# A mixed fp32 block kernel on one core: k's values and squares interleaved by transfers, one pass of products for the k features, and a new order of each batch on every engine

## The reference

```python
mod = (silu(c) @ wmod).reshape(16, 6, 1, 128)        # sa, ca, ga, sb, cb, gb of each batch
h = layernorm(x) * (1 + ca) + sa
# attention with 16 heads of 8 dimensions and M = 32 random features:
#   feature(u) = (exp(u @ orf.T / 8**0.25 - sum(u*u) / (2*8**0.5)) + 1e-6) / sqrt(32)
q, k = feature(h @ Wq.T + bq), feature(h @ Wk.T + bk);  v = h @ Wv.T + bv
out = q @ (k.T @ v) / (q @ sum(k))                    # per batch and head
x = x + ga * (out @ Wo.T + bo)
h = layernorm(x) * (1 + cb) + sb
e = argmax(h @ gate_W + gate_b)                       # one of 8 experts for each row
x = x + gb * (gelu(h @ W1[e] + b1[e]) @ W2[e] + b2[e])
```

## Time and profile before

| | |
|---|---|
| device time, median of 3 runs | 381.62 us (381.19 to 385.29) |
| span of the profiled execution | 360.6 us |
| median less that span | 21.0 us |
| TensorE busy with matmuls, share of the span | 94% |
| TensorE weight loads | 73% |
| VectorE, ScalarE, GpSimd | 75%, 74%, 59% |
| bytes moved by transfers | 60.47 MB, 168 GB/s |

### The profile page before, as it was taken

One profiled execution on the slowest core, in us unless ns is written; L12 is line 12 of the kernel. 1 busy time (PEld: TensorE's weight loads), 2 busy tenths in 40 slices (PEclk: granted clock), 3 DMA queues, 4 the chain that ended last, 5 costly groups with the idle time before them and its releaser, 6 DMA issues.

```text
span 360.6 us, 13729 instructions
## 1 busy us (share of the span) xinstructions
PE 338.8 (94%) x4823; PEld 263.9 (73%) x4823; DVE 271.2 (75%) x1104; ACT 265.1 (74%) x644; POOL 213.2 (59%) x262
## 2 busy tenths in 40 slices
PE   6899999899988999998999999999999999999994
PEld 5445765566465566646665669999989999999993
DVE  3456997898879789878887978887677676666653
ACT  2688988799878888977888756676656667666761
POOL 3142386776667757857854618846767455545554
PEclk9999999999999999999999999999999999999999
DMA  7174656774566547444432467445657665545410
GB/s 233 50 253 166 210 184 221 259 243 160 177 227 205 176 167 230 163 132 156 153 133 100 149 163 227 142 118 150 194 161 269 209 184 147 147 128 135 137 38 12
DMA packets 40211, 60.47 MB, mean 168 GB/s; under 512 B 5426, under 2 KB 28086, under 8 KB 40016
## 3 DMA queue, kind: packets, MB, share of 16 engines
q1 hardware_dynamic: 33776, 42.54, 39.9%
q0 software_dynamic: 6368, 17.05, 12.5%
HBM read 28.63 MB, written 19.34 MB: 133 GB/s over the span
## 4 chain that ended last, share of the span: by engine, by line
PE 60%; ACT 15%; DMA 10%; DVE 6%; issue 5%; POOL 1%; SPq 1%; DVEq 1%; POOLq 0%; ACTq 0%
PE ps_proj L1350 16%; PE ps_feat L1337 9%; DMA qmix<-qsqs 9%; PE ps_proj L1132 6%; PE ps_den_gate L1337 4%; PE ps_proj L1182 4%; PE ps_kv L1337 4%; ACT qf L627 3%; ACT qvals L606 2%; ACT shared L588 2%; PE ps_kv L1198 2%; PE ps_out L1330 2%; ACT den L656 2%; ACT shared L581 2%; ACT kvm L600 2%
## 5 line engine op out<-in xcount | busy, mean ns | idle before, releaser
L545 POOL DMA_INDIRECT out<-kf,modb x71 | 70.1, 987 | 52.4 <-DVE kf L1060 47.0
L507 POOL DMA_INDIRECT experts_lists<-pay,slot x64 | 65.9, 1030 | 43.4 <-DVE slot L893 29.5
L1350 PE MATMUL ps_proj<-w2sb,qf 128*128 x568 | 75.0, 275 | 0.4 <-ACT qf L690 0.4
L1350 PEld LDWEIGHTS ps_proj<-w2sb,qf 128*128 128x128 f32 x568 | 68.9, 192 | 0.6 <-issue 0.6
L681 ACT ACTIVATE xT<-ps_out 128x128 f32<-128x128 f32 x71 | 19.7, 277 | 44.8 <-PE ps_out L1330 44.1
L1055 DVE TENSOR_TENSOR kf<-ps_proj,firsts_sb 128x128 f32<-128x128 f32 x71 | 20.7, 291 | 34.6 <-PE ps_proj L1350 22.6
L690 ACT ACTIVATE qf<-ps_feat,shared 128x128 f32<-128x128 f32 x144 | 40.9, 374 | 0.0
L1337 PE MATMUL ps_feat<-xT,shared 128*128 128x128 f32 x288 | 38.8, 277 | 1.5 <-issue 0.9
L1337 PEld LDWEIGHTS ps_feat<-xT,shared 128*128 128x128 f32 x288 | 35.0, 192 | 2.8 <-issue 1.7
L1132 PE MATMUL ps_proj<-shared,wsb 128*128 128x512 f32 x62 | 33.3, 620 | 1.0 <-ACT shared L581 0.4
L977 DVE COPY shared<-firsts_sb 128x516 f32 x71 | 31.4, 442 | 1.6 <-issue 1.5
(11 more groups left out here) (189 smaller groups left out, 890.3 us busy)
## 6 DMA issues: line engine op xcount, KB each, us to landing
modb<-experts_lists SPq DMA_DIRECT2D x71, 196.0 KB, 2.8
xall<-in_x SPq DMA_DIRECT2D x16, 256.0 KB, 3.0
pay<-modb SPq DMA_DIRECT2D x16, 256.0 KB, 3.0
qmix<-qvals SPq DMA_DIRECT2D x30, 128.0 KB
qmix<-qsqs SPq DMA_DIRECT2D x30, 128.0 KB
modb<-modulation_rows SPq DMA_DIRECT2D x4, 768.0 KB, 5.2
firsts_sb<-in_firsts SPq DMA_DIRECT2D x8, 322.0 KB, 4.2
w2sb<-in_w SPq DMA_DIRECT2D x8, 256.0 KB
```

What stands on the lines that cost most here:

```text
L507: g_.indirect_dma_start(out=lists, in_=pay[b.home][:, t, :], in_offset=None, out_offset=bass.IndirectOffsetOnAxis(ap=slot[b.home][:, t:t + ...
L545: g_.indirect_dma_start(out=rows_out, in_=yb[u], in_offset=None, out_offset=bass.IndirectOffsetOnAxis(ap=token, axis=0), bounds_check=last ...
L1350: ins = mm(Y[u % 2][:, 0:D], g[u % R4][:, c * P:(c + 1) * P], w2sb[:, bass.ds(e * DFF + c * D, D)], start=(c == 0), stop=(c == FC - 1))
```

## The change

- k's weights are permuted as q's are, ACT's `kvals` and `ksqs` are interleaved by four transfers (`mix_k(v)` on SP) into a new buffer `kmix`, and `k_features` makes 32 products of 64 columns, 32 partitions x 128 rows stationary, in one pass. Batch 0 keeps the two passes.
- k of batch b is projected into G (for b from 2 on), the bank of den. The projection waits for the attention of batch b-2, and the transpose of kvT into G waits for k's values and squares.
- v of batch b is projected and copied in turn b-1.
- Each engine's turn has a new order, in POOL's `rstd1_of` goes first, in SP's turn v `mix_k(v)` stands first and `mix_q(v)` last, behind `gate_rows(v)` and `load_w2`. The rest of POOL's turn is as before.
- The last batch has its own lists.

```diff
@@ sync
             for v in range(1, B):
-                mix_q(v)
+                mix_k(v)
                 if v + EARLY_ROWS + 1 < B:
                     load_x_behind(v + EARLY_ROWS + 1)
...
                     gate_rows(v)
                 if 5 <= v < 5 + E:
                     load_w2(v - 5)
+                mix_q(v)
+            def mix_k(v):
+                sp.wait_ge(s_kst, 2 * v + 1)
+                for n in range(2):
+                    sp.dma_start(kmix[n::2, n, :], kvals[n::2, :]).then_inc(s_kmix, 16)
+                sp.wait_ge(s_kst, 2 * v + 2)
+                for n in range(2):
+                    sp.dma_start(kmix[1 - n::2, n, :], ksqs[n::2, :]).then_inc(s_kmix, 16)
@@ gpsimd
+                if ahead and b.par == 0:
+                    rstd1_of(b.half + 3, b=b + 2)
                 if not first:
                     rstd2_of(b + -1, rows_of=None if second else b + -2)
-                if ahead and b.par == 0:
-                    rstd1_of(b.half + 3, b=b + 2)
@@ scalar, the turn of a middle batch
+                k_pair(b, 0)
+                modulate(b + 1)
+                k_pair(b, 1)
+                if not second:
+                    h2T_copy(b + -2)
+                k_values(b + 1)
+                k_squares(b + 1)
+                q_pair(b, 0)
+                if not second:
+                    gateT(b + -2)
+                q_pair(b, 1)
+                kvm_copy(b)
+                v_values(b + 1)
+                q_values(b + 1)
+                q_squares(b + 1)
+                rden_first(b)
                 if b.v + 2 < B:
                     normalise1(b + 2)
@@ vector, the whole turn of a middle batch as it now stands (statistics of x ahead of it)
                 residual(b + -1)
                 second_stats(b + -1)
                 centre_h2(b + -1)
                 kv_values(b, first)
                 normalise1(b + 2, lo=LT // 2)
                 experts(b + -2)
                 eps_values(b)
                 scale_h2(b + -1)
                 slots(b + -2)
                 attention(b)
@@ tensor
+            def k_features(b):
+                pe.wait_ge(s_kmix, 64 * b.v)
...
+                for t in range(LT):
+                    for n in range(2):
+                        for c in range(NC):
+                            at = slice(c * CW, (c + 1) * CW)
+                            ins = mm(QB[c][:, t * P + n * HP:t * P + (n + 1) * HP], kmix[at, n, t * P:(t + 1) * P],
+                                     feat_q[at, n, :], start=True, stop=True)
@@ tensor, the turn of a middle batch
+                k_features(b)
+                if not second:
+                    transpose_h2(b + -2, first=b.v == 2)
+                transpose_xn(b + 1)
+                out_project(b + -1)
+                project_k(b + 1)
+                q_features(b)
+                kv_product(b)
+                if not second:
+                    gate(b + -2)
+                project_v(b + 1)
+                kv_transpose(b)
+                if not second:
+                    gate_transpose(b + -2)
+                project_q(b + 1)
+                eps_and_den(b)
+                if not second:
+                    rank(b + -2, first=b.v == 2)
+                numerator(b)
```

More of the change, by code:

```diff
@@ L635, in gateT, with rden_first @@
                 a.activation(lgT[:], I[:, 0:P], ACT.Copy).then_inc(s_lgT, 1)
[L637 to L653, removed]
+            def rden_first(b):
                 act.wait_ge(s_den, b.v + 1)
@@ L658, in batch, with first_batch, last_batch @@
                 a.activation(rden[:], den[:], ACT.Exp, scale=-1.0).then_inc(s_rden, 1)
-                if not last:
-                    q_squares(b + 1)
+            def first_batch(b):
+                k_pair(b, 0)
+                k_pair(b, 1)
+                v_values(b)
+                q_pair(b, 0, first=True)
+                modulate(b + 1)
+                q_pair(b, 1, first=True)
+                k_values(b + 1)
[5 more added lines that the diff above has]
+                rden_first(b)
+                normalise1(b + 2)
+            def last_batch(b):
+                k_pair(b, 0)
+                h2T_copy(b + -2)
+                k_pair(b, 1)
+                gateT(b + -2)
+                q_pair(b, 0)
+                q_pair(b, 1)
+                kvm_copy(b)
+                rden_first(b)
+            def batch(b, first=False, second=False, last=False, ahead=True):
+                if first:
+                    return first_batch(b)
+                if last:
+                    return last_batch(b)
+                k_pair(b, 0)
+                modulate(b + 1)
+                k_pair(b, 1)
+                if not second:
+                    h2T_copy(b + -2)
+                k_values(b + 1)
+                k_squares(b + 1)
+                q_pair(b, 0)
+                if not second:
+                    gateT(b + -2)
+                q_pair(b, 1)
+                kvm_copy(b)
+                v_values(b + 1)
+                q_values(b + 1)
+                q_squares(b + 1)
+                rden_first(b)
                 if b.v + 2 < B:
@@ L1001, in batch @@
                     second_stats(b + -1)
+                if second:
+                    dve.wait_ge(s_mb, 16)
+                if b.v > EARLY_ROWS and (b.v - 1 - EARLY_ROWS) % LATE_ROWS == 0:
+                    dve.wait_ge(s_mbl, 16 * ((b.v - 1 - EARLY_ROWS) // LATE_ROWS + 1))
+                if not first and not last:
+                    centre_h2(b + -1)
                 if last:
                     table_rows(0)
-                    kv_values(b)
+                kv_values(b, first)
+                if last:
                     experts(b + -2)
@@ L1008, in batch @@
                     copy_firsts(0)
-                elif not first and not second:
+                if b.v + 2 < B:
+                    normalise1(b + 2, lo=LT // 2)
+                if not first and not second and not last:
                     experts(b + -2)
[L1011 to L1018, removed]
                 eps_values(b)
                 if not first and not last:
-                    centre_h2(b + -1)
                     scale_h2(b + -1)
+                if not first and not second and not last:
+                    slots(b + -2)
                 if b.v == B - 2:
@@ L1140, in v_project, with first_k_features @@
                              start=True, stop=True)
[L1141 to L1149, removed]
+                ins.then_inc(s_pv, 1)
+            def first_k_features(b):
+                pe.wait_ge(s_kst, 2)
                 for t in range(LT):
@@ L1278, in batch @@
             def batch(b, first=False, second=False, last=False, ahead=True):
-                third = b.v == 2
+                if first:
+                    return first_batch(b)
                 if last:
[L1281 to L1288, removed]
+                    return last_batch(b)
@@ L1289, in batch @@
+                k_features(b)
+                if not second:
+                    transpose_h2(b + -2, first=b.v == 2)
+                transpose_xn(b + 1)
+                out_project(b + -1)
+                project_k(b + 1)
+                q_features(b)
+                kv_product(b)
+                if not second:
                     gate(b + -2)
-                q_features(b, first)
-                if not first and not second:
+                project_v(b + 1)
+                kv_transpose(b)
```

138 lines of the change are left out of this document (83 added, 55 removed).

## The result

The changed kernel takes 535.88 us (534.52 to 537.39) against 382.63, a ratio of 1.400 (95% interval 1.392 to 1.409): 153 us slower, where 170 were forecast.

A forecast was written before the change was run, and what follows sets the result against it. TensorE, busy for 338.8 of 360.6 us, was taken as the bound. Loop 151, clock 19, start 3, less 2 of idle time, sum to 171 us; 381.6 + 171 = 553, stated as 552, range 520 to 590.

The forecast's parts named there:

- The step that decides: SP's order: `mix_q` behind `gate_rows` and its scatter wait makes a loop, 151 us over the turns v = 3 to 15.
- The terms of the round: Stretches from one `q_features` through eps product, slots, scatter, `gate_rows` and q's transfers to the next: 24.3 us against 12.4.
- from the squares to `q_features`: Transfer of q's squares, from their issue on SP to TensorE's use of them: 4.54 us per turn.
- The range: Whole kernel: 520 to 590 us, from the ends of the scatter-to-`gate_rows` stretch, q's transfers and the clock.
- Step 6: End of the round: issue of q's values 1.2 us, then squares to `q_features` 4.54; 4.1 to 5.9 in all.
- the low ends: Smallest values of the uncertain terms in the 13 stalled turns: a turn costs 10.7 us more.
- The clock: TensorE falls to 1.2 GHz in each stall and loses 1.5 us: 13 x 1.5 = 19 us, between 0 and 39.
- The k pass: TensorE's k products take 1.8 us instead of 2.1, paced by stationary loads; gain 0.3 per turn, at most 1.1.
- The start and end: Turn 1 loses 3 us to uncovered k transfers; turns 1 and 2 may lose 1 us of idle time each.
- Span and median: The 21.0 us between profiled span and median time were left as they are for the changed kernel.
- The rival of the orders alone: SP's wait is harmless and wo paces the new order: 0.3 to 2 us per turn, 385 to 410; chance 0.03.

The follow-up runs named there:

- before_qmix_last: The kernel before with only `mix_q` moved last in SP's turn, behind `gate_rows` and `load_w2`: 507.86 us, ratio 1.322.
- qmix_first: The changed kernel with `mix_q` moved right behind `mix_k`, ahead of the wait of `gate_rows` for the scatter: 432.81 us, ratio 1.124.
- before_again: The kernel before, unchanged, profiled again beside the others: one execution, 388.19 us, span 386.3.
- gates_later: As qmix_first, with `gate_rows` one turn later, for batch v-1 in SP's turn v: 404.52 us, ratio 1.054.
- gated_first: As gates_later, with POOL making wo ahead of all four scatters instead of behind two: 403.18 us, ratio 1.054.
- slots_earlier: As gates_later, with DVE's `slots` ahead of `scale_h2`: 378.71 us beside 362.45 of the kernel before, ratio 1.044.
- wide_again: keep_warm_wide once more, on one chip with narrow_again: 518.58 us beside 383.79 of the kernel before, ratio 1.345.
- narrow_again: The changed kernel with 150 idle products of 128 columns in the stall, repeated beside wide_again: 527.62 us, ratio 1.376.
- keep_warm_wide: The changed kernel with 39 idle products of 512 columns in the stall: 491.53 us beside 362.45 of the kernel before, ratio 1.353.

## Why the prediction was right

**The step that decides** was right as it stood: `mix_q` behind the wait of `gate_rows`, 13 stalls, a loop through slots, scatters and the last tile. before_qmix_last makes 124 of the 153 us with that line alone, qmix_first takes 103 away with it.

**The terms of the round**, forecast and measured in the round shown: eps product 4.9 plus 1.5 for the clock, measured 6.6 (4.5 when the clock holds), then 2.8 to slots for my 2.8; tile 3 at 14.1 plus 1.5, measured 15.8; to `gate_rows` 3.1, measured 2.6; `gate_rows` and `load_w2` 1.34 and 1.35; q's values 1.2 and 1.2; from the squares to `q_features` 4.54, measured 2.87. This last is the mis-sized one. I took it from a single turn of the kernel before, and a long one: over the 14 turns of that profile it is 3.25 to 4.79, 3.9 on average. Loads of x and of the experts' weights and TensorE's work stood beside that transfer; which of them made it longer was not separated. It takes 1.7 x 13 = 22 us off the sum, and the landing of the scatter another 0.5 x 13 = 6.

**The range.** Step 6 measured 1.23 + 2.87 = 4.1, which is the low end that I gave it. But the turn at the low ends, 10.7 us over the one before, doesn't follow from these ends: 11.6 less 0.5 and 1.6 is 9.5, and the range should have begun near 506. It did no harm, as the measured turn is 10.9 to 11.4 over, by which steps it is counted.

**The clock** fell as said. It costs 2.1 us per turn, 27 us, against 19 forecast, within the bounds. The 1.5 us was a guess that a row only half supports: the pace of products at the start was low for 3 us, but the granted clock of those windows is 1.00. In the stalls it is 0.50 for at least 3 us behind `q_features`, and in four of the 13 turns for 5. Filling the stall gave back up to 5.5% of the kernel before (1.400 to 1.345), about 21 us.

**The k pass**: forecast 1.8, measured 1.94 without gaps, and no gain from half the columns. That the gain would be 0.3 per turn was too much, it is 0.06. In 11 of its 15 turns the changed kernel's pass has gaps and takes 2.4 to 3.5 us; under the stall this costs nothing.

**The start and end**: 3 us less 2 us forecast, 9.0 measured up to `q_features` of batch 2. TensorE waits 3.2 us for k's transfers in turn 1, the cost that I named, and 2.6 for q's in turn 2; what makes up the rest I did not separate.

**Luck.** The errors went both ways: transfer and landing took 28 us off, the clock and the start put 8 each back. So 552 came nearer to 536 than its terms deserved.

**Span and median.** I carried 21.0 us between span and median over to the changed kernel. It was not overhead around the span, which is 1.8 us (537.39 and 535.6), but a second phase of 152 us in the profiled execution and, by before_again, some 173 in such timed ones. It did no harm only because the change does not touch that phase.

**The rival of the orders alone** (0.3 to 2 us per turn, 385 to 410) is the size of what gates_later shows once both loops through SP are gone: 1.2 us per turn, and 5 at the start, 1.054. As a rival to the forecast it fell. That wo behind late slots makes this rest is not shown: with wo ahead of the scatters it stayed (gated_first), and slots_earlier did not move the slots. The four more transfers are in it as well. None of the versions beats the kernel before, and these traces show nothing that the change could win: its pass over k takes as long as the one before (1.94 against 2.00).

## What to carry to other kernels

Before moving an instruction in an in-order list, look at what each entry that it is moved behind waits for, on the queue that issues transfers above all: its waits were free only as long as nothing urgent stood behind them. Then follow the wait round to its source; if it leads back to the moved step's own result of one turn earlier, the turn becomes as long as the way round. And the k products here, 128 stationary and 64 or 128 moving columns, were paced by their stationary loads (1.94 and 2.00 us a pass): to shorten such a pass, try fewer or narrower loads, not fewer moving columns.

## What the runs showed of the hardware that was not expected

- Transfers of q took 2.9 us from the issue of the squares to use with TensorE still, and, in the turns in which they ended the stall, 3.2 with 39 wide and 4.0 with 150 narrow idle products beside them (wide_again, narrow_again), and 2.8 in most turns of keep_warm_wide, where the kernel before took 362 us. What delays them is not settled.
- The same kernel takes 362 us beside some runs and 384 beside others, and its second phase 152 or 174 us in the profiles. In the longer form TensorE's stream also has gaps that the profile puts down to no wait: its k pass takes 2.3 to 3.4 us in all but three turns of before_again, 2.0 in the first profile. One chip gave both times (384.24 beside qmix_first, 362.45 beside keep_warm_wide), so the chip alone doesn't explain it. Why is open.
